# First layer's weights in three transfers behind x, its small vectors issued by ScalarE

## What is computed

```python
def _L0_xattn_ref(hidden_states, encoder_states, ltor_mask, cross_mask, ...):
    ln_out = layernorm(hidden_states, ln1_s, ln1_b)
    qkv = ln_out @ w_qkv + b_qkv
    q, k, v = jnp.split(qkv, 3, axis=-1)
    ctx = merge_heads(attention(split_heads(q), split_heads(k), split_heads(v), ltor_mask))
    attn_out = ctx @ w_ao + b_ao
    x = hidden_states + attn_out
    ...            # cross attention over encoder_states, then a gelu MLP
```

## Time and profile before

| | |
|---|---|
| median of 3 runs | 2168.41 us (2166.06 to 2172.05) |
| the profiled execution, its own time | 2155.11 us |
| its span, first to last instruction | 2153.4 us |
| mean granted TensorE clock | 0.954 |
| PE busy | 1940.0 us (90%) |
| VectorE busy | 1437.3 us (67%) |
| ScalarE busy | 867.1 us (40%) |
| bytes moved | 234.90 MB, mean 109 GB/s |

### The profile page before, as it was taken

One profiled execution on the slowest core, in us unless ns is written; L12 is line 12 of the kernel. 1 busy time (PEld: TensorE's weight loads), 2 busy tenths in 40 slices (PEclk: granted clock), 3 DMA queues, 4 the chain that ended last, 5 costly groups with the idle time before them and its releaser, 6 DMA issues.

```text
span 2153.4 us, 28651 instructions
## 1 busy us (share of the span) xinstructions
PE 1940.0 (90%) x11012; PEld 1334.3 (62%) x11012; DVE 1437.3 (67%) x2431; ACT 867.1 (40%) x2024; POOL 523.9 (24%) x245
## 2 busy tenths in 40 slices
PE   5789999999999997999998999999999997885456
PEld 4566666666666664676775767757667656563233
DVE  3366667666666542122778787878878878999942
ACT  2466666666666743222312423414224213130221
POOL 1233334333343321020302202204104023130100
PEclk9799999999999998999999999999999998897687
DMA  7000010000001113544538437446365453443221
GB/s 207 25 1 25 11 35 21 16 25 11 26 14 71 40 64 98 203 139 153 188 113 271 150 125 253 148 147 219 115 191 191 137 197 108 156 137 119 90 78 49
DMA packets 155215, 234.90 MB, mean 109 GB/s; under 512 B 24152, under 2 KB 72024, under 8 KB 155080
## 3 DMA queue, kind: packets, MB, share of 16 engines
q1 hardware_dynamic: 138184, 216.28, 30.3%
q10 hardware_dynamic: 16896, 16.80, 2.3%
HBM read 191.09 MB, written 41.96 MB: 108 GB/s over the span
## 4 chain that ended last, share of the span: by engine, by line
PE 42%; DVE 7%; DMA 3%; ACT 2%; issue 2%; POOL 2%; SPq 1%; POOLq 0%; DVEq 0%; ACTq 0%
PE b_f_bank L1747 9%; PE b_a_bank L1770 9%; PE b_f_bank L1737 7%; PE b_c_bank L1780 6%; PE b_a_bank L1789 4%; DVE b_ring L1982 3%; PE b_c_bank L1770 3%; DMA b_o<-b_o_all 2%; PE b_y_bank L1809 2%; DVE b_ring L1971 1%; PE b_c_bank L1789 1%; PE b_f_bank L1897 1%; POOL b_mixed L1656 1%; DVE b_ring L1989 1%; DMA k_w_early<-in_w_dram 1%
## 5 line engine op out<-in xcount | busy, mean ns | idle before, releaser
L401 POOL TENSOR_TENSOR a_prob<-a_prob,a_rowinv 128x1024 f32<-128x1024 f32 x128 | 242.2, 1893 | 507.8 <-DVE a_rowinv L854 507.8
L1982 DVE TENSOR_TENSOR_SCAN b_ring<-b_ws,b_ring 128x1028 f32<-128x1028 f32 x128 | 354.0, 2806 | 6.1 <-ACT b_ring L2194 3.2
L1086 ACT ACTIVATE a_prob<-a_score,a_low 128x256 f32<-128x256 f32 x512 | 253.6, 497 | 226.5 <-DVE a_low L846 226.5
L1656 POOL TENSOR_TENSOR b_mixed<-b_mixed,b_xaT 128x1024 f32<-128x1024 f32 x40 | 119.9, 2998 | 606.6 <-DVE b_mixed L1999 606.5
L1747 PE MATMUL b_f_bank<-k_w_early 128*128 128x512 f32 x448 | 204.1, 603 | 12.3 <-DMA k_w_early<-in_w_dram 8.1
L1737 PE MATMUL b_f_bank<-k_hT_early,k_w_early 128*128 128x256 f32 x896 | 205.0, 385 | 6.5 <-ACT b_xaT L2174 5.7
L846 DVE CUSTOM_DVE_ANT_0 a_score<-a_score,a_fill 128x256 f32<-128x256 f32 x512 | 196.6, 447 | 4.8 <-DVE a_score L833 0.3
L1737 PEld LDWEIGHTS b_f_bank<-k_hT_early,k_w_early 128*128 128x128 f32 x896 | 169.3, 192 | 36.0 <-issue 14.0
L833 DVE SCALAR_TENSOR_TENSOR a_score<-a_S,a_mask 128x1024 f32<-128x1024 f32 x128 | 150.7, 1219 | 48.2 <-PE a_S L595 48.2
L1770 PE MATMUL b_a_bank<-b_mixed,b_shared 128*128 128x256 f32 x768 | 172.7, 382 | 4.4 <-POOL b_mixed L1656 3.2
L826 DVE TENSOR_SCALAR a_ctxT<-a_O,a_vec 128x256 f32<-128x256 f32 x64 | 31.0, 484 | 208.7 <-PE a_O L625 208.7
(11 more groups left out here) (162 smaller groups left out, 3053.1 us busy)
## 6 DMA issues: line engine op xcount, KB each, us to landing
k_w_early<-in_w_dram SPq DMA_DIRECT2D x64, 1024.0 KB, 5.3
b_vs<-b_v_all SPq DMA_DIRECT2D x32, 512.0 KB, 6.1
b_shared<-in_Wv_dram SPq DMA_DIRECT2D x8, 1024.0 KB, 5.5
b_shared<-in_Wk_dram SPq DMA_DIRECT2D x8, 1024.0 KB, 6.0
b_shared<-in_Wg_dram SPq DMA_DIRECT2D x8, 1024.0 KB, 7.5
b_shared<-in_Wo_dram SPq DMA_DIRECT2D x8, 1024.0 KB, 10.3
b_shared<-in_Wfv_dram SPq DMA_DIRECT2D x8, 1024.0 KB, 6.6
b_shared<-in_Wfk_dram SPq DMA_DIRECT2D x8, 1024.0 KB, 5.6
```

The source lines that it names most:

```text
L401: nc.gpsimd.tensor_tensor(two, two, inv.to_broadcast([P, 2 * TT, SEQ]), ALU.mult)\
L1086: last = nc.scalar.activation(prob[:, slot, a * SEQ:(a + 1) * SEQ], score[:, j, a * SEQ:(a + 1) * SEQ], ACT.Exp, bias=low[:, head, a:a + 1 ...
L1656: nc.gpsimd.tensor_tensor(mixed[:, f % 2, :, :], mixed[:, f % 2, :, :], xaT[:, :, 1:SEQ + 1], ALU.add)\
L1982: last = nc.vector.tensor_tensor_scan(x_, flat(ws[:, :, :]), x_, 0.0, ALU.mult, ALU.add)
```

## The change

Four edits, all in the prologue of `attention_block`:

1. SP no longer issues the ten vectors. ACT issues them, as its first instructions.
2. `w_qkv` comes in three transfers (query, key, value columns, 1 MB each, rows of 2 KB), each with a semaphore; they stand on SP's queue directly behind x. PE waits for each part ahead of the first product that uses it.
3. ACT's wait for the vectors moves from ahead of the root to behind it, ahead of `hidden_self(0)`.
4. Behind the issues and the wait for the constants, ACT takes a root of one column (`warm`), whose result nothing reads.

```diff
--- before.py
+++ after.py
@@ -102,6 +102,7 @@
         meanvar = sb("meanvar", P, TT, 2)
         std = sb("std", P, TT)
         rstd = sb("rstd", P, TT)
+        warm = sb("warm", P, 1)
 
         S = psum("S", HPG, TT * SEQ)
         O = psum("O", 512)
@@ -137,7 +138,7 @@
 
         vectors_in = sem("vectors_in")
         self_mask_in = sem("self_mask_in")
-        w_qkv_in = sem("w_qkv_in")
+        w_qkv_in = [sem(f"w_{name}1_in") for name in "qkv"]
         weights_in = sem("weights_in")
         biases_in = sem("biases_in")
         consts_made = sem("consts_made")
@@ -351,10 +352,10 @@
 
             x_out.prime(sp)
             load_x(0)
-            with nc.allow_non_contiguous_dma(reason="channel vectors, once"):
-                for name, i in vi.items():
-                    sp.dma_start(vec[:, i, :], T[name].rearrange("(c p) -> p c", p=P)).then_inc(vectors_in, 16)
-            sp.dma_start(w_qkv[:, :, :], T["w_qkv"].rearrange("(c p) n -> p c n", p=P)).then_inc(w_qkv_in, 16)
+            for i in range(3):
+                sp.dma_start(w_qkv[:, :, i * DM:(i + 1) * DM],
+                             T["w_qkv"].rearrange("(c p) n -> p c n", p=P)[:, :, i * DM:(i + 1) * DM])\
+                    .then_inc(w_qkv_in[i], 16)
             sp.dma_start(mask[:, 0, :].rearrange("p (a k) -> p a k", a=TT),
                          T["mask_self"].rearrange("(a p) k -> p a k", p=P)).then_inc(self_mask_in, 16)
             load_enc(0)
@@ -757,12 +758,14 @@
 
             first = Filler(Turn(-1, ("next",), ()))
             first.hidden_self(0)
-            pe.wait_ge(w_qkv_in, 16)
+            pe.wait_ge(w_qkv_in[0], 16)
             first.self_q(0)
+            pe.wait_ge(w_qkv_in[1], 16)
             first.self_k(0)
             scores((0, 0, 0))
             first.self_q(1)
             first.self_k(1)
+            pe.wait_ge(w_qkv_in[2], 16)
             for k in range(TT):
                 first.self_v(k)
             run_iterations(pe, iteration)
@@ -1019,8 +1022,11 @@
 
         @block.scalar
         def _(act):
-            act.wait_ge(vectors_in, 16 * N_VECTOR_DMAS)
+            with nc.allow_non_contiguous_dma(reason="channel vectors, once"):
+                for name, i in vi.items():
+                    act.dma_start(vec[:, i, :], T[name].rearrange("(c p) -> p c", p=P)).then_inc(vectors_in, 16)
             act.wait_ge(consts_made, 2)
+            nc.scalar.activation(warm[:, :], eps_col[:, :], ACT.Sqrt, bias=eps_col[:, :])
 
             def root(d, st):
                 act.wait_ge(var_made[st].sem, var_made[st].at(d, 1))
@@ -1173,6 +1179,7 @@
                 softmax(7)
 
             root(0, "next")
+            act.wait_ge(vectors_in, 16 * N_VECTOR_DMAS)
             hidden_self(0)
             self_k(0, 0)
             for j in range(HPG):
```

## The result

The change makes the kernel slower: median 2181.81 us over 7 runs (2173.25 to 2183.78), against 2166.06 (2163.1 to 2172.05) for the kernel before over as many. The ratio is 1.0064, 95% interval 1.0048 to 1.0080: 13.9 us (10.4 to 17.3); the two medians taken by themselves lie 15.8 us apart. The forecast was 2185.4, which was 17.0 over the median of before as it was known then, 2168.4.

A forecast was written before the change was run, and what follows sets the result against it. PE bounds the kernel, busy 1940.0 of 2153.4 us, so a delay before its first product moves everything. hT1, waiting for the vectors, makes that product 17.0 us later: 2168.4 + 17.0 = 2185.4 us, range 2168 to 2196.

The forecast's parts named there:

- What ended last before, and what the split would do: Kernel start: w_qkv ends last, 4.0 us over hT1; split, its query part lands by about 7.5 us, hT1 is late next.
- One packet for one: DMA queues of SP and ACT: turns go by packets, not bytes, so one vector packet passes per weight packet; chance 0.50.
- (a): Rival, vectors' DMA: small packets pass in bunches, vectors land at 8.8 us, first product 4.3 us earlier, 2164.1 us; chance 0.16.
- (d): Rival, vectors' DMA: turns of two to three small packets, vectors at 15 to 22 us, 2168 to 2173 us; chance 0.07.
- (b): Rival, DMA queues: turns by partition or whole transfer, vectors land at 24.5 us, product 8.9 us later, 2177.3 us; chance 0.18.
- 330 against 298 packets, the bulk's end at 30.2 to 32.9: Per engine, ten vectors' 330 packets outnumber SP's 298, so the last passes after the bulk, ending at 30.2 to 32.9 us.
- The price of a small packet beside large ones: Vector packets between the bulk's: add nothing at least, at most 330 x 8.3 ns = 2.7 us.
- (c): Rival, vectors' DMA: 4-byte packets cost 46 ns each, 330 add 15 us instead of 2.7, up to 2197.7 us; chance 0.09.
- ACT held in its issues: ACT's tenth vector issue is held by its full queue until near 20 us; root at about 22 instead of 8.90.
- A late start of ACT's queue: ACT's DMA queue starts 2 us late behind what SP issued before; counted with the rival of costlier small packets, chance 0.09.
- Nothing downstream gives it back: After the first query product: next transfers are triggered by products and move along, so the 17.0 us reach the end.
- The 0.3 us that root and wait would give: Prologue on ACT: extra root and moved wait start the real root at 8.6 instead of 8.9 us, if issues aren't held.

The follow-up runs named there:

- the first version: Changed kernel with no vectors on ACT: SP issues x, four prologue vectors, three w_qkv parts, then six vectors; ratio 0.9974 against before, 0.9973 once more.

## Why the prediction was right

- **What ended last before, and what the split would do.** Right: w_qkv held the product by 4 us, and with the split alone it comes 3.6 us earlier.
- **One packet for one.** Right, and the forecast rests on it. It was read from two queues with 1 and 2 KB rows and held for 4-byte packets against 1, 2 and 4 KB. Rivals (a) and (d), bunches of small packets, are out by the counts above, and with them the rule of several to a turn that was cited under (a). So is (b), turns by partition or by transfer: that would have landed the vectors at 24.5, and given two vector packets for each of the mask's, which has two rows to a partition.
- **330 against 298 packets, the bulk's end at 30.2 to 32.9.** SP's queue passed 4715 packets up to 32 us, 295 per engine, and the last vector packet passed at about 32.1. The copies began at 32.66, where 32.6 was forecast. The agreement is better than the steps deserve, and in part luck. In the first microseconds it was not one for one: the 35 packets per engine that q10 was ahead by 8 us were the surplus of 32 that I had put behind the bulk's end. And x, with the vectors beside it, passed its last packets at about 4.9 instead of 3.9, so the bulk began 1 us later than I took, while the packets between added less than half of what I allowed at most (the next point).
- **The price of a small packet beside large ones.** Taken at up to 8.3 ns from the packets alone. From 8 to 10 us a packet was in work for 0.121 x 2 x 16 / 353 = 11.0 ns, but in part at the same time as the large ones: the two shares add up to 110%. What it added to the bulk is less. The bulk took from 4.9 to 32.2 us for what it had carried from 8.2 to 34.2 before (from 0.5 to 10.15 MB in both), 27.3 instead of 26.0 us. That is about 4 ns for each of the 330, an estimate that holds the cost of the shorter rows of w_qkv too. Rival (c), 46 ns, is out.
- **ACT held in its issues.** Right as a mechanism, its size off: the end of the tenth issue was put near 20 us and was 17.60, the root at about 22 and was at 19.12. The depth that I took, 120 packets per engine, was about right at that point (some 3170 of 5280 had passed by then, which leaves 130 per engine), and so was the pair's 90 ns (2 x 16 / 353 us is 91). The even pace that I assumed from the start was the error, by the same head start. It is no firm depth, though: counted the same way, 130 to 160 per engine were outstanding when the sixth to the ninth issue ended. The error cost nothing, as hT1 waited for the vectors anyway.
- **A late start of ACT's queue.** The earlier trace rows were read as ACT's packets waiting for what SP had issued before them. The changed kernel shows such a stretch only from 5.5 to 6.5 us; after that the two take turns. That reading carried none of the forecast, and no run tests it.
- **Nothing downstream gives it back.** Right: 17.0 us at the first product, and 13.9 (10.4 to 17.3) and 17.8 (11.9 to 23.4) at the end. In each of the eleven comparisons of this document the shift of the first product, from 6.4 us earlier to 20.7 later, lies inside the interval of the end. The forecast 2185.4 is 3.6 us over the measured median, and its 17.0 us lie just inside the first interval. Part of the 3.6 is the median of before itself, 2166.06 over 7 runs and 2168.4 over the 3 known then.
- **The 0.3 us that root and wait would give** never came, as the issues held ACT; without them and with the split they are worth 1.7 us at the first product (14.08 with the split alone, 12.38 with both).
- **The Trainium skill** (DMA: Bandwidth & Descriptors, "Issuing engines are not separate DMA queues") has the two queues interleave on the same engines; the trace agrees, 353 packets beside 353. That a second issuer saves its issue time held for SP, whose weights went out 5.8 us earlier (1.36 instead of 7.16), but not for both engines together: ACT spent 16.8 us (0.80 to 17.60) on what had cost SP 5.8.

## What to carry to other kernels

Before a transfer of many tiny elements is moved to another queue, count packets, not bytes: beside a full queue it got one turn per packet of the other here, so it landed when as many large packets had gone. Tiny transfers that something early waits for belong ahead of the bulk on the same queue, and only those; the rest can follow. And the issuing engine was held with some 110 to 160 packets per DMA engine of its queue outstanding (an estimate from the counts at the ends of the held issues: SP's before, ACT's in the changed kernel and with the vectors on ACT alone), so such transfers should not stand at the head of an engine that has early work of its own.

## What was not expected of the hardware

- The first 16 query products took between 5.23 and 6.55 us in these profiles, the next 16 some 3.7, while the windows over them give a granted clock of 1.00. Their length after an idle stretch varies from execution to execution: the changed kernel's two profiles have 5.70 and 6.55 us. Whether the edits have a part in it isn't shown (6.41 us with the root alone, 5.23 before), nor why they are slow at that clock.
- The steps of the lag. The two profiles of the first version with four vectors ahead, same code, have spans of 2168.0 and 2154.8 us, though their first products lie 0.2 us apart. The one step that is looked at here is a stand of 1 to 2 us with slower products at a lower granted clock behind it. A single profile's span is then no measure of a change of 0.3%; the place of the first product is.
- x itself landed 0.9 us later (statistics at 5.61 instead of 4.70), with the vectors' packets beside it from the start. In all profiles with vectors on ACT it is 5.55 to 5.69, in all others 4.54 to 4.98.
